# One ACT and one DVE instruction for both masks of a channel tile

## The chip, the cores and the metric

The kernel runs on one core of a Trainium2 chip. The metric is the device time of one execution in microseconds (us); lower is better. The engines have short names: PE is TensorE, DVE is VectorE, ACT is ScalarE, POOL is GpSimd, SP is SyncE.

## The reference

A block of a network with adaptive layer norm: a Mamba-2 layer over 1024 tokens and 512 features, then a small projection with signed weights. Only the part that the change touches matters here. The 1024 tokens are cut into chunks of 128, and the layer has 128 heads of 64 channels in 8 groups.

```python
A_cum = jnp.cumsum(A_dt, axis=-1)
L = jnp.exp(_segsum(A_dt))            # per head and chunk, 128 x 128, lower triangle
Y_diag = jnp.einsum('bzlhn,bzshn,bhzls,bzshp->bzlhp', Cc, Bc, L, xch)
...
Y_off = jnp.einsum('bzlhn,bzhpn,bhzl->bzlhp', Cc, prev, jnp.exp(A_cum))
Y = (Y_diag + Y_off).reshape(b, s, H, P) + hs * D[None, None, :, None]
g = y * jax.nn.silu(gate)
```

For each head the mask exp(A_cum[l] - A_cum[s]) is multiplied by C B^T, which all heads of a group share, and the product multiplies the scaled inputs.

## The kernel before

**Work and stages.** The kernel has 32 units: 8 groups (g), and in each of them four units c = 0 to 3. A unit is a block of 512 channels (8 heads) times half of the tokens (512, which is 4 chunks): c = 0 and 1 are the first block of the group, c = 2 and 3 the second; even c is the first half of the tokens (hf = 0), odd c the second. The first and the last group are written out, and groups 1 to 6 are one loop. Every engine has its own program in which the order of the work is written out by hand, and semaphores tie the programs together.

**The first part of a unit.** TensorE makes the gate projections (gate_proj, L638), transposes the inputs (L717) and makes the chunk states and the output projection of the unit before. A gate projection has to wait for the convolution of the channels before it (v_conv) and, for z = 2, for an earlier SiLU of a gate (a_gate), which frees the PSUM bank.

**The second part, where the change is.** It runs over the four channel tiles j of the unit, two heads each. For tile j:

- PE: exp_a(j) (L692) spreads exp(A_cum) into a bank, diff(2j) and diff(2j+1) (L677) put the differences of A_cum in banks 2 and 3. These run one tile ahead. Then come C times the states (L801, "yo") which waits for v_t1 of tile j-1, and the masked product (L814, "yd") which waits for v_m. For tile 0 it waits also until the part sum of the unit before is read out of its bank (L1340 or L1343). After it come input projections (L488 to L490) for the next unit.
- ACT: ea(j) (L1100), a copy out of PSUM that for j >= 2 waits for POOL's sum of tile j-2 (p_t3). Then decays(j) (L1086): two Relu (L1092) that take the two differences out of PSUM to lm, and two Exp in place (L1095). After it come g_hi and the square of tile j-1, one step of the convolution (L920), a weight part (L890), and at the end of the unit the SiLU of the next inputs (L1037) and gates (L1050).
- DVE: mix (L1430) multiplies lm of a head by cbm, the masked C B^T. Then t2(j) (L1460, `yt`) and t1(j) (L1465, `ea`), g_lo of tile j-1 (L1442) and the convolution (L1241). The mixes of tile j+1 stand ahead of t2 and t1 of tile j.
- POOL: for tile j the sum (L1634, waits for t1(j)), the product with the gate (L1637), the sum of squares (L1629) and the low part of a weight (L1549).

lm has four slots of 512 columns, so the two heads of a tile lie next to each other: slots 0 and 1 for even j, 2 and 3 for odd j.

Of the kernel before, what the change touches and what calls it, by code (L numbers as in the profile page):

```python
# [15 lines left out]
HALF = 512  # L16
# [9 lines left out]
def adaln_mamba_ffn(nc: bass.Bass, x, w_in, w_out, blk_par, bc_par, dt_bias, a_log, c_col, w_mod,  # L26
                    w_ffn, b_ffn, ident_in, keep_in, rows_in, cols_in, sel_in, out):
    F, R, BF = mybir.dt.float32, mybir.dt.float32r, mybir.dt.bfloat16
    ALU, ACT = mybir.AluOpType, mybir.ActivationFunctionType

    ctx = ExitStack()
    with ctx:
        def sb(name, shape, dt=F):
            return ctx.enter_context(nc.sbuf_tensor(name, shape, dt))

        def sem(name):
            return ctx.enter_context(nc.semaphore(name))
# [12 lines left out]
        lm = sb("lm", [128, 4, HALF])  # L50
# [9 lines left out]
        cbm = sb("cbm", [128, TOK])  # L60
# [26 lines left out]
        def scratch(name, shape, dt=F):  # L87
# [24 lines left out]
                   for i in range(2)]  # L112
# [15 lines left out]
        a_silu, a_bcsilu, a_l = sem("a_silu"), sem("a_bcsilu"), sem("a_l")  # L128
        a_fall, a_ea, a_hi, a_sq = sem("a_fall"), sem("a_ea"), sem("a_hi"), sem("a_sq")
# [3 lines left out]
        v_cbm, v_bl, v_m, v_t1, v_t2, v_lo = (sem("v_cbm"), sem("v_bl"), sem("v_m"), sem("v_t1"), sem("v_t2"),  # L133
                                              sem("v_lo"))
# [4 lines left out]
        def ge(eng, s, value):  # L139

            if not (isinstance(value, int) and value <= 0):
                eng.wait_ge(s, value)


        def toks(hf, z=0, n=NZ):
            return slice(hf * HALF + z * CHUNK, hf * HALF + (z + n) * CHUNK)

        def chunk(z):
            return slice(z * CHUNK, (z + 1) * CHUNK)

        def slot(hf, z):

            return (NZ * hf + z) % (NZ + 1)
# [21 lines left out]
        def par(b, j, k):  # L175

            i = j * (TAPS + 3) + k
            return bpar[:, b, i:i + 1]
# [5 lines left out]
        def flat(t, a, b):  # L184

            return t[:, a:b, :].rearrange("p a n -> p (a n)")
# [88 lines left out]
        def late_bank(z):  # L275

            return (7, 0, 1)[z - 1]
# [204 lines left out]
        def _(te):  # L482
# [167 lines left out]
            def unit(g, c, last, first):  # L650
                u, nb, hf = UPG * g + c, 2 * g + c // 2, c % 2
# [28 lines left out]
                def exp_a(j):  # L680

                    if j == 0:
                        te.wait_ge(d_par[par_], 208 * (nb + 1))
                    if j == 0:
                        te.wait_ge(a_gate, 4 * u + 3)
                    elif j == 1:
                        if not first:
                            out_read(g, c, 0 if end else 2)
                    else:
                        te.wait_ge(a_ea, 4 * u + j)  # L690
                    e = 32 * EA_ROWS[j]
                    nc.tensor.matmul(bank[ea_bank(c, j)][:, :], sel[e:e + SROWS, :], rt[par_][e:e + SROWS, :],  # L692
                                     start=True, stop=True).then_inc(t_ea, 1)
# [92 lines left out]
                for j in range(NCT):  # L786
                    if j < NCT - 1:
                        exp_a(j + 1)
                        diff(2 * j + 2)
                        diff(2 * j + 3)  # L790

                    if j == 0:
                        te.wait_ge(v_prev, sb0 + 3)
                        if c in (0, 3):
                            ge(te, v_var, 2 * g + (1 if c else 0))
                        if c == 0:
                            te.wait_ge(v_bl, 2 * g + 1)
                    else:
                        te.wait_ge(v_t1, 4 * u + j)
                    for z in range(1 - hf, NZ):  # L800
                        lst = nc.tensor.matmul(bank[6][:, chunk(z)], prev[:, slot(hf, z), j * 128:(j + 1) * 128],  # L801
                                               ct[:, toks(hf, z, 1)], start=True, stop=True)
                    lst.then_inc(t_yo, 1)

                    te.wait_ge(v_m, 8 * u + 2 * j + 2)
                    if j == 0:
                        if not end and not first:
                            out_read(g, c, 3)
                    else:
                        te.wait_ge(v_t2, 4 * u + j)  # L810
                    for z in range(NZ):
                        for i in range(2):
                            h = 2 * j + i
                            lst = nc.tensor.matmul(bank[5][64 * i:64 * i + 64, chunk(z)],  # L814
                                                   xdt[:, z, h * HDIM:(h + 1) * HDIM], lm[:, h % 4, chunk(z)],
                                                   start=True, stop=True)
                    lst.then_inc(t_yd, 1)
                    if j == 0:
                        n = project_step(0, 0)
                    if j >= 1 and end:  # L820
                        if j >= 2:
                            te.wait_ge(v_row, 2)
                        out_proj(u - 1, j, late_bank(j))
                    if j == 0 and end:

                        te.wait_ge(a_gate, 4 * UNITS)
                        for v in range(2):
                            for k in range(NK):
                                te.wait_ge(v_diag, NK * v + k + 1)
                                lst = nc.tensor.matmul(bank[v][:, k * 128:(k + 1) * 128], ones[:, :],  # L830
                                                       (ga_row, gb_row)[v][:, k * 128:(k + 1) * 128],
                                                       start=True, stop=True)
                            lst.then_inc(t_row, 1)
                    n = project_step(j + 1, n)
                    if j == 2 and c < 3:
                        gate_proj(g, c + 1, 0)
# [13 lines left out]
            u = UNITS - 1  # L850
# [33 lines left out]
        def _(se):  # L884
            act = nc.scalar.activation
# [176 lines left out]
            def unit(g, c, last, first):  # L1062
                u, nb, hf = UPG * g + c, 2 * g + c // 2, c % 2
# [22 lines left out]
                def decays(j):  # L1086


                    for h in (2 * j, 2 * j + 1):
                        se.wait_ge(t_diff, 8 * u + h + 1)  # L1090
                        ge(se, t_yd, 4 * u + h // 2 - 1)
                        act(lm[:, h % 4, :], bank[2 + h % 2][:, :], ACT.Relu, scale=-1.0).then_inc(a_fall, 1)  # L1092
                    for h in (2 * j, 2 * j + 1):
                        se.wait_ge(a_fall, 8 * u + h + 1)
                        act(lm[:, h % 4, :], lm[:, h % 4, :], ACT.Exp, scale=-1.0).then_inc(a_l, 1)  # L1095

                def exp_a(j):
                    se.wait_ge(t_ea, 4 * u + j + 1)
# [83 lines left out]
        def _(ve):  # L1182
            vec = nc.vector
            tt, stt, ts = vec.tensor_tensor, vec.scalar_tensor_tensor, vec.tensor_scalar
# [140 lines left out]
            two = lambda t: t.rearrange("p (v k) -> p v k", v=2)  # L1325
# [39 lines left out]
            def unit(g, c, last, first):  # L1365
                u, nb, hf = UPG * g + c, 2 * g + c // 2, c % 2
# [60 lines left out]
                nv, hv = (nb, 1) if hf == 0 else (nb + 1, 0)  # L1427
                pv = (c // 2) if hf == 0 else (c // 2 + 1) % 2

                def mix(h):  # L1430

                    ve.wait_ge(a_l, 8 * u + h + 1)
                    if h == 0 and c == 0:
                        ve.wait_ge(v_cbm, 2 * g + 2)
                    tt(lm[:, h % 4, :], lm[:, h % 4, :], cbm[:, toks(hf)], ALU.mult).then_inc(v_m, 1)  # L1435

                def lower_g(j):
                    ve.wait_ge(a_hi, 4 * u + j + 1)
# [4 lines left out]
                        ALU.mult, ALU.subtract).then_inc(v_lo, 1)  # L1443

                mix(0)
                mix(1)
                if not first and not end:
                    accumulate(u, g1, b1, h1, 3)
                if hf == 0:
# [1 line left out]
                cols = slice(0 if hf else CHUNK, HALF)  # L1451
                for j in range(NCT):
                    if j < NCT - 1:
                        mix(2 * j + 2)
                        mix(2 * j + 3)

                    ve.wait_ge(t_yd, 4 * u + j + 1)
                    ge(ve, a_sq, 4 * u + j - 1)
                    ge(ve, v_lo, 4 * u + j - 1)
                    stt(yt[:, j % 2, :], xc[:, j, :], par(c // 2, j, SKIP), bank[5][:, :], ALU.mult, ALU.add)\  # L1460
                        .then_inc(v_t2, 1)

                    ve.wait_ge(t_yo, 4 * u + j + 1)
                    ve.wait_ge(a_ea, 4 * u + j + 1)
                    tt(ea[:, j % 2, cols], bank[6][:, cols], ea[:, j % 2, cols], ALU.mult).then_inc(v_t1, 1)  # L1465
                    if j >= 1:
                        lower_g(j - 1)
                    for item in items[j]:
                        conv(item, item_bank(n), nv, hv, g + 1, pv)
                        n += 1  # L1470
                    if end:
                        if j == 0:
                            gate_rows()
                        else:
                            accumulate(u, g1, b1, h1, j, late_bank(j))
                        for t in ((), (), (0,), (1,))[j]:
                            first_residual(t)
# [244 lines left out]
```

## Time and profile before

| what | value |
|---|---|
| median of 3 runs | 1830.39 us (1828.36 to 1834.19) |
| the profiled execution | 1830.74 us |
| its span, first to last instruction | 1828.9 us |
| granted TensorE clock, mean over the span | 0.985 |
| PE busy | 1740.6 us, 95% |
| DVE busy | 1309.0 us, 72% |
| ACT busy | 1014.8 us, 55% |
| POOL busy | 945.9 us, 52% |

Durations and waits come from the profiled execution, which lies 0.35 us above the median; 1.84 us of it lie outside the span. A start time is counted from the first instruction. In the rows, "idle before" or a bracket is the time in which the engine had nothing to run before this instruction, and the arrow names what ended it.

### The profile page before, as it was taken

The page shows a single profiled execution, that of the slowest core. Times are in us where ns is not written, and L with a number is a line of the kernel's source. Part 1 is how long each engine was busy: PE and PEld are TensorE (multiplying, and loading weights), DVE is VectorE, ACT ScalarE, POOL GpSimd, SP SyncE. Part 2 cuts the span into 40 slices and gives each one's busy share as a digit, 9 for nine tenths or more (in the row PEclk, how much of TensorE's full clock was granted, in tenths as well). Part 3 has the DMA queues.
Part 4 walks back from the last instruction along what each step waited for, and adds up shares of the span by engine and source line. Part 5 has one row for each costly group of instructions (what it writes and reads, how often), then busy time and mean ns, then how long its engine had stood idle before and what let it go on. Part 6 is the DMA issues. An engine that isn't in the chain of part 4 may idle for free.

```text
span 1828.9 us, 31129 instructions
## 1 busy us (share of the span) xinstructions
PE 1740.6 (95%) x9656; PEld 1332.9 (73%) x9656; DVE 1309.0 (72%) x2175; ACT 1014.8 (55%) x1709; POOL 945.9 (52%) x723
## 2 busy tenths in 40 slices
PE   6789999999999999999999999999999999999966
PEld 5567777777777777777777777777777777777745
DVE  4766677667866677766777678666777667766788
ACT  6566554565646565565545656465656655565532
POOL 1355464555536465454645555355654546455563
PEclk9899999999999999999999999999999999999988
DMA  6312121121202121121211212121211212111131
GB/s 226 106 39 67 61 67 44 48 63 53 73 28 67 50 71 52 31 68 60 67 45 48 63 53 70 31 73 44 72 52 30 73 56 67 44 50 61 35 98 58
DMA packets 80784, 112.65 MB, mean 62 GB/s; under 512 B 28384, under 2 KB 32480, under 8 KB 79712
## 3 DMA queue, kind: packets, MB, share of 16 engines
q1 hardware_dynamic: 63040, 78.50, 14.1%
q10 hardware_dynamic: 17568, 31.99, 5.2%
q8 instruction: 88, 1.44, 0.3%
q14 instruction: 88, 0.72, 0.1%
HBM read 88.16 MB, written 22.29 MB: 60 GB/s over the span
## 4 chain that ended last, share of the span: by engine, by line
issue 46%; POOL 33%; PE 11%; DVE 4%; ACT 3%; DMA 1%; SPq 1%; POOLq 1%; ACTq 0%; DVEq 0%
POOL yt L1634 9%; POOL ssq L1629 6%; POOL wg_lo L1549 4%; POOL prev L1615 3%; POOL wo_lo L1549 3%; POOL wx_lo L1549 3%; PE bank L488 3%; POOL yt L1637 3%; PE bank L490 2%; PE bank L489 2%; PE bank L663 1%; PE bank L729 1%; DMA raw_w<-w_in_dram 1%; PE bank L862 1%; DMA gate<-w_mod_dram 0%
## 5 line engine op out<-in xcount | busy, mean ns | idle before, releaser
L1634 POOL TENSOR_TENSOR yt<-yt,ea 128x384 f32<-128x384 f32 (+1 forms) x128 | 189.4, 1480 | 392.4 <-DVE ea L1465 392.4
L1435 DVE TENSOR_TENSOR lm<-lm,cbm 128x512 f32<-128x512 f32 x256 | 186.7, 770 | 169.3 <-ACT lm L1095 169.3
L1241 DVE SCALAR_TENSOR_TENSOR xc<-bank,bpar,xc 128x511 f32<-128x511 f32 (+2 forms) x384 | 285.9, 745 | 6.8
L488 PE MATMUL bank<-h_hi,wg_hi 128*128 128x512 f32 x640 | 262.9, 411 | 21.6 <-ACT gate L1050 9.2
L490 PE MATMUL bank<-h_hi,wg_lo 128*128 128x512 f32 x640 | 251.8, 393 | 0.0
L489 PE MATMUL bank<-h_lo,wg_hi 128*128 128x512 f32 x640 | 250.7, 392 | 0.0
L488 PE MATMUL bank<-h_hi,wx_hi 128*128 128x512 f32 x512 | 210.5, 411 | 2.2 <-DVE bt L1241 2.2
L1615 POOL TENSOR_TENSOR prev<-prev,dec 128x512 f32<-128x512 f32 x96 | 102.0, 1062 | 204.6 <-DVE prev L1381 132.0
L488 PE MATMUL bank<-wo_hi,g_hi 128*128 128x512 f32 x496 | 206.6, 417 | 0.0
L490 PE MATMUL bank<-h_hi,wx_lo 128*128 128x512 f32 x512 | 200.5, 392 | 0.0
L489 PE MATMUL bank<-h_lo,wx_hi 128*128 128x512 f32 x512 | 199.8, 390 | 0.0
L490 PE MATMUL bank<-wo_hi,g_lo 128*128 128x512 f32 x496 | 194.7, 393 | 0.0
L489 PE MATMUL bank<-wo_lo,g_hi 128*128 128x512 f32 x496 | 193.5, 390 | 0.0
L1050 ACT ACTIVATE gate<-bank 128x512 f32<-128x512 f32 x128 | 75.2, 588 | 208.4 <-PE bank L490 97.4
L1100 ACT ACTIVATE ea<-bank 128x512 f32<-128x512 f32 x128 | 76.4, 597 | 183.0 <-PE bank L692 132.8
L1637 POOL TENSOR_TENSOR yt<-yt,gate 128x512 f32<-128x512 f32 x128 | 165.9, 1296 | 10.0
L488 PEld LDWEIGHTS bank<-h_hi,wg_hi 128*128 128x128 f32 x640 | 121.0, 189 | 64.2 <-ACT gate L1050 14.3
L920 ACT ACTIVATE xc<-bank,bpar 128x512 f32<-128x512 f32 (+1 forms) x128 | 99.2, 775 | 112.2 <-PE bank L490 64.0
L1095 ACT ACTIVATE lm<-lm 128x512 f32<-128x512 f32 x256 | 149.0, 644 | 0.0
L1629 POOL TENSOR_TENSOR ssq<-ssq,sq 128x512 f32<-128x512 f32 x112 | 145.4, 1298 | 2.6 <-ACT sq L1119 2.6
L814 PE MATMUL bank<-lm,xdt 128*64 128x128 f32 x2048 | 140.6, 280 | 5.4 <-DVE part L1343 4.4
L1549 POOL TENSOR_TENSOR wg_lo<-raw_w,wg_hi 128x512 fp32r<-128x512 f32 x80 | 112.9, 1411 | 56.4 <-ACT wg_hi L890 56.2
(192 smaller groups left out, 3693.6 us busy)
## 6 DMA issues: line engine op xcount, KB each, us to landing
raw_w<-w_in_dram SPq DMA_DIRECT2D x145, 256.0 KB, 2.6
raw_w<-w_out_dram SPq DMA_DIRECT2D x64, 256.0 KB, 2.6
part_d<-part ACTq DMA_DIRECT2D x64, 256.0 KB, 2.0
part<-part_d ACTq DMA_DIRECT2D x58, 256.0 KB, 2.7
rt<-rows_d SPq DMA_DIRECT2D x256, 6.0 KB
acc<-x_dram SPq DMA_DIRECT2D x8, 256.0 KB, 6.9
acc<-w_mod_dram SPq DMA_DIRECT2D x2, 1024.0 KB, 6.7
lh<-neg_d SPq DMA_DIRECT2D x128, 6.0 KB
```

Source lines behind the costliest of these rows:

```text
L488: nc.tensor.matmul(out_ap, whi(k), hhi(k), start=(k == 0), stop=False)
L489: nc.tensor.matmul(out_ap, whi(k), hlo(k), start=False, stop=False)
L490: last = nc.tensor.matmul(out_ap, wlo(k), hhi(k), start=False, stop=(k == n - 1))
L814: lst = nc.tensor.matmul(bank[5][64 * i:64 * i + 64, chunk(z)], xdt[:, z, h * HDIM:(h + 1) * HDIM], lm[:, h % 4, chunk(z)], start=True, st ...
L1095: act(lm[:, h % 4, :], lm[:, h % 4, :], ACT.Exp, scale=-1.0).then_inc(a_l, 1)
L1241: stt(dst[:, at], ps[:, 0:HALF - 3 + k], w(k), dst[:, at], ALU.mult, ALU.add)\
L1435: tt(lm[:, h % 4, :], lm[:, h % 4, :], cbm[:, toks(hf)], ALU.mult).then_inc(v_m, 1)
L1549: tt(lo[:, j, :], raw_w[:, s, :], hi[:, j, :].bitcast(F), ALU.subtract).then_inc(p_w, 1)
L1615: tt(prev[:, slot(hf, z + 1), :].rearrange("p (h c) -> p h c", h=BH), prev[:, slot(hf, z), :].rearrange("p (h c) -> p h c", h=BH), d.unsqu ...
L1629: tt(ssq[:, hf, :], ssq[:, hf, :], sq[:, :], ALU.add).then_inc(p_ss, 1)
L1634: tt(yt[:, j % 2, cols], yt[:, j % 2, cols], ea[:, j % 2, cols], ALU.add).then_inc(p_t3, 1)
L1637: tt(yt[:, j % 2, :], yt[:, j % 2, :], gate[:, j, :], ALU.mult).then_inc(p_g, 1)
```

## The change

The two Exp of a tile become one instruction over 1024 columns (both slots of lm), which waits for both Relu. The two products with cbm become one instruction over 2 x 512 columns, in which cbm is read twice by a stride of zero. The semaphores a_l and v_m count one per tile in place of two. The Relu, the number of slots and the order of all the rest stay.

```diff
-                    te.wait_ge(v_m, 8 * u + 2 * j + 2)
+                    te.wait_ge(v_m, 4 * u + j + 1)
...
-                    for h in (2 * j, 2 * j + 1):
-                        se.wait_ge(a_fall, 8 * u + h + 1)
-                        act(lm[:, h % 4, :], lm[:, h % 4, :], ACT.Exp, scale=-1.0).then_inc(a_l, 1)
+                    at = flat(lm, 2 * j % 4, 2 * j % 4 + 2)
+                    se.wait_ge(a_fall, 8 * u + 2 * j + 2)
+                    act(at, at, ACT.Exp, scale=-1.0).then_inc(a_l, 1)
...
-                def mix(h):
+                def mix(j):
-                    ve.wait_ge(a_l, 8 * u + h + 1)
-                    if h == 0 and c == 0:
+                    ve.wait_ge(a_l, 4 * u + j + 1)
+                    if j == 0 and c == 0:
                         ve.wait_ge(v_cbm, 2 * g + 2)
-                    tt(lm[:, h % 4, :], lm[:, h % 4, :], cbm[:, toks(hf)], ALU.mult).then_inc(v_m, 1)
+                    two = lm[:, 2 * j % 4:2 * j % 4 + 2, :]
+                    tt(two, two, cbm[:, toks(hf)].unsqueeze(1).broadcast_to((128, 2, HALF)), ALU.mult).then_inc(v_m, 1)
...
                 mix(0)
-                mix(1)
...
-                        mix(2 * j + 2)
-                        mix(2 * j + 3)
+                        mix(j + 1)
```

## Rows read from the trace of the kernel before

**Rows 1.** The page, part 1: busy time and share of each engine.
```profile
PE 1740.6 (95%) x9656; PEld 1332.9 (73%) x9656; DVE 1309.0 (72%) x2175; ACT 1014.8 (55%) x1709; POOL 945.9 (52%) x723
```

**Rows 2.** Waits of PE over the span: us in total, times, longest.
```profile
PE bank L488 <- ACT gate L1050: 9.2, 20, 2.3
PE bank L488 <- DVE xc L1241: 7.2, 9, 1.0
...
PE bank L814 <- DVE part L1343: 4.4, 7, 0.8
...
PE bank L801 <- DVE ea L1465: 4.0, 3, 2.0
```

**Rows 3.** ACT's timeline, a unit c = 1: start us, us, instruction, idle before.
```profile
1017.24 0.60 ACT L1100 ACTIVATE ea<-bank 128x512 f32<-128x512 f32 x1 [1.12 <-PE bank L692]
1017.74 1.08 ACT L1092 ACTIVATE lm<-bank 128x512 f32<-128x512 f32 x2
1018.69 1.16 ACT L1095 ACTIVATE lm<-lm 128x512 f32<-128x512 f32 x2
...
1023.80 0.60 ACT L1100 ACTIVATE ea<-bank 128x512 f32<-128x512 f32 x1 [1.15 <-POOL yt L1634]
...
1025.25 1.16 ACT L1095 ACTIVATE lm<-lm 128x512 f32<-128x512 f32 x2
```

**Rows 4.** DVE's timeline, the same unit.
```profile
1009.28 0.68 DVE L1340 COPY part<-bank 128x512 f32<-128x512 f32 x1
...
1019.36 1.29 DVE L1435 TENSOR_TENSOR lm<-lm,cbm 128x512 f32<-128x512 f32 x2 [1.50 <-ACT lm L1095]
1020.57 0.74 DVE L1460 SCALAR_TENSOR_TENSOR yt<-xc,bpar,bank 128x512 f32<-128x512 f32 x1
...
1025.93 1.55 DVE L1435 TENSOR_TENSOR lm<-lm,cbm 128x512 f32<-128x512 f32 x2 [0.94 <-ACT lm L1095]
```

**Rows 5.** Groups of instructions by line: count, busy us and mean ns, idle before.
```profile
L1095 ACT ACTIVATE lm<-lm 128x512 f32<-128x512 f32 x256 | 149.0, 644 | 0.0
...
L1041 ACT ACTIVATE bt<-bt 128x1024 f32<-128x1024 f32 x8 | 8.5, 1064 | 0.1
...
L1435 DVE TENSOR_TENSOR lm<-lm,cbm 128x512 f32<-128x512 f32 x256 | 186.7, 770 | 169.3 <-ACT lm L1095 169.3
...
L1241 DVE SCALAR_TENSOR_TENSOR xc<-bank,bpar,xc 128x511 f32<-128x511 f32 (+2 forms) x384 | 285.9, 745 | 6.8
...
L1227 DVE SCALAR_TENSOR_TENSOR xc<-bank,bpar,tail 128x3 f32<-128x3 f32 x64 | 13.7, 214 | 15.8 <-ACT xc L920 15.8
```

**Rows 6.** ACT's timeline at the start: an instruction that waits for the one before it.
```profile
19.14 0.78 ACT L929 ACTIVATE yt<-bank,modc 128x512 f32<-128x512 f32 x1 [0.91 <-PE bank L507]
19.95 0.63 ACT L932 ACTIVATE h_hi<-yt 128x512 fp32r<-128x512 f32 x1
```

**Rows 7.** POOL's timeline, the unit of rows 3.
```profile
1022.00 1.71 POOL L1634 TENSOR_TENSOR yt<-yt,ea 128x512 f32<-128x512 f32 x1 [2.93 <-DVE ea L1465]
```

**Rows 8.** PE's timeline, the unit of rows 3.
```profile
1010.12 1.09 PE L814 MATMUL bank<-lm,xdt 128*64 128x128 f32 x16
...
1035.55 0.50 PE L488 MATMUL bank<-h_hi,wg_hi 128*128 128x512 f32 x1 [0.30 <-ACT gate L1050]
```

**Rows 9.** Timeline of all engines at the end of a unit c = 0.
```profile
986.08 0.58 ACT L1050 ACTIVATE gate<-bank 128x512 f32<-128x512 f32 x1
...
986.72 0.50 PE L488 MATMUL bank<-h_hi,wg_hi 128*128 128x512 f32 x1
```

**Rows 10.** Timeline of all engines, tile 3 of a unit c = 2.
```profile
1075.20 2.66 DVE L1435 TENSOR_TENSOR lm<-lm,cbm 128x512 f32<-128x512 f32 x2 [0.59 <-ACT lm L1095]
...
1075.56 1.75 POOL L1549 TENSOR_TENSOR wo_lo<-raw_w,wo_hi 128x512 fp32r<-128x512 f32 x1
...
1082.19 0.50 PE L488 MATMUL bank<-h_hi,wg_hi 128*128 128x512 f32 x1 [0.86 <-DVE xc L1241]
```

**Rows 11.** PE's timeline, tile 0 of a unit c = 3.
```profile
1110.42 1.09 PE L814 MATMUL bank<-lm,xdt 128*64 128x128 f32 x16 [0.61 <-DVE part L1343]
```

## The prediction

> **What bounds the kernel now.** I read the page's busy shares first: PE is busy 95% of the span, no other engine over 72% [rows 1]. ACT and DVE time saved is thus worth nothing by itself; what counts is when PE is made to wait. The list of PE's waits shows few, and they repeat group by group [rows 2]: for a gate's SiLU (20 times), for a convolution (9 times), for the read-out of the part sum ahead of the masked product (7 times), and in the last unit for t1. Then the timelines of one group, engine by engine, to see what each wait hangs on. In a unit c = 1 [rows 3, 4, 7, 8] the chain is:
>
> PE's diff(2) -> ACT's ea(2), Relu pair, Exp pair -> mixes of tile 2 -> t2(1), t1(1) -> POOL's sum (it had waited 2.93 us for t1) -> ea(3) (it had waited 1.15 us for POOL) -> Relu, Exp -> mixes of tile 3 (0.94 us of waiting for Exp) -> t2(2), t1(2) -> POOL's next sum, product and squares -> ACT's g_hi, square, gate -> PE's gate projection, which waits 0.30 us [rows 8].
>
> The end of a unit is therefore bound by a chain of latencies that passes two Exp and mix pairs, and PE has no slack there. The other units end alike: c = 0 has gate ready at 986.66 and PE starts at 986.72 [rows 9]; c = 2 waits 0.86 us for the convolution behind the same t1(2) [rows 10].
>
> **The change, step by step.** All from an Exp pair's present start, X.
>
> *Now.* The Relu pair starts 0.95 before X (1017.74 and 1018.69) and ends 0.13 after it. The first Exp doesn't need the second Relu, so it starts before that has ended. The first mix starts at X + 0.67 (1019.36), while the second Exp runs; the next DVE instruction starts 1.21 later (1020.57), at X + 1.88 [rows 3, 4].
>
> *After.* The Exp must wait for the second Relu: X + 0.13, plus 0.03 for a wait on the engine's own result (19.14 + 0.78 to 19.95 [rows 6]). It has 1024 columns; the trace has no such Exp, only a SiLU of that size at 1064 ns [rows 5], and I take 1.07. The pair now takes 1.16 [rows 3], an upper bound; 1.05 is my lower one. The mix starts 0.03 later, at X + 1.26. No DVE product of 1024 columns is there either: 745 ns for 511 columns and 214 for 3 make 1.045 ns a column [rows 5]. A pair takes 1.29 and holds the engine 1.21, each mix thus 0.69 and holds it 0.605 [rows 4]; with 0.535 more for 512 columns the merged mix holds it 1.14 (bounds 1.10, and 1.21 if nothing is saved). So the next DVE instruction starts at X + 2.40.
>
> The saving in occupancy is 0.07 on DVE and about 0.09 on ACT, which there goes into the 0.16 for the second Relu. The price is that nothing overlaps: each pair that DVE waits for hands on **0.52 us later** (bounds 0.43 and 0.68). Most pairs are such: DVE waits 169.3 us for this Exp, 1.3 us for each of 128 pairs [rows 5]. Behind the waiting mix stand, in DVE's queue, the part sum's read-out (tile 0), t2 and t1 (the others), so it is they that come late.
>
> What passes to PE, at each place:
>
> 1. End of unit, c = 0 and c = 1: t1(1), POOL's sum and ea(3) come 0.52 later, then Exp at 1025.25 + 0.52, and t2(2) at 2.40 behind it, 1028.17. Now it is 1025.93 + 1.55 - 0.08 = 1027.40 (this pair was held up 0.26 by POOL) [rows 3, 4]. That is 0.77, and PE already waits, or is within 0.06 of it: 16 x 0.77 = 12.3 us.
> 2. c = 2: the pair takes 2.66, for POOL works at the same time [rows 10]. With everything 0.52 later POOL's wo_lo starts at 1076.08, ahead of the merged mix (ready at 1075.20 - 0.67 + 0.52 + 1.26 = 1076.31), which I let wait for POOL's end, 1.29 later: free for t2 at 1077.40 + 1.14 = 1078.54 against 1075.20 + 2.66 - 0.08 = 1077.78. That is 0.76, 8 x = 6.1. Were it not held up, t2 would start at 1077.45, 0.33 earlier than now. Both ends count below.
> 3. Masked product of tile 0, c = 3: PE waits for the part sum, which stands behind the mix [rows 2, 11]: 7 x 0.52 = 3.6. For c = 1 the same read-out ends at 1009.96, 0.16 before PE's product at 1010.12 [rows 4, 8]; at 1009.96 + 0.52 + 0.04 it makes PE wait 0.40: 8 x 0.40 = 3.2.
> 4. End of c = 3: DVE is full of convolutions from tile 2 on, so one pair costs 0.52 and the next gives 0.06 back: 0.46, seven times 3.2. Whether PE feels all of it at the turn of the loop is open (bound 0).
> 5. Once in the first unit, where the masked product waits for the mix, 0.5; the last unit, without projections to hide anything, waits for t1 at tiles 2 and 3 [rows 2]: two passed pairs, 1.1.
>
> Places 1 and 3 add up, since the later chain starts from a later PE. Where PE waits at none of these places, the delay is hidden by the input projections between two masked products (over 4 us each). The DMAs, counts of semaphores and PE's own work stay. Sum: 12.3 + 6.1 + 3.6 + 3.2 + 3.2 + 1.6 = **30.0 us**. On the profiled 1830.74 us that is 1860.7, and on the median, 0.35 lower, 1860.4; I say 1860.
>
> **What the Trainium skill says to this.** A DVE product of two SBUF operands and a POOL instruction hold each other up [rows 10]: the pair takes 2.66 us in place of 1.29. The Trainium skill ("SBUF — State Buffer", section "SBUF: two separate sides") has this as an exclusive lock: who starts first keeps the port pair for its whole instruction. By it place 2 costs 6.1 us; without such a lock it would be 8 x -0.33, and the sum 21. The Trainium skill also says in "Perfetto Trace Analysis", section "Optimizing Scalar/DVE Operations", that larger instructions help a saturated engine, and that where these engines aren't saturated but make others wait, breaking instructions up may let work be done sooner; here neither is saturated and PE waits for them, so it speaks against the change. The sum stands without it.
>
> **Rivals.**
>
> *POOL doesn't hold up the mix of c = 2 (chance 0.20).* Place 2 turns to 8 x -0.33 = -2.6 in place of 6.1, and place 4 is not felt: 30.0 - 8.7 - 3.2 = 18.1, 1848.5. For it: POOL's wo_lo and the mix are only 0.23 us apart there. Against: the same chain delays both, so their order should be the same each time.
>
> *The long mix collides more (0.08).* A mix takes 770 ns on the mean against 690 unhindered [rows 4, 5], so 20 us are lost to POOL now. If a merged mix that holds on twice as long meets a POOL instruction of 1.29 us in each of the 16 ends of place 1, 21 us more come on top: 1881. Against: by my times POOL is free when those mixes are ready.
>
> *Occupancy decides (0.04, faster).* PE's waits are set by how full DVE is. Then the 24 unit ends and 7 read-outs of places 1 to 3 get back two pairs at 0.07 each: 4.3 us, 1826. It decides where DVE has no idle time ahead of a mix; yet it is idle there for 169.3 us in sum [rows 5]. The Trainium skill ("Perfetto Trace Analysis", "Optimizing Scalar/DVE Operations") has such a gain from grouping for a saturated engine only, which by the trace DVE is at tile 3 of c = 3 alone.
>
> *Hidden delay (0.08, on the other side: no change).* If PE's short waits are an artefact of modelled matmul ends, and it has 1 us of slack at the ends of units, 0.77 is swallowed: 1830 to 1832. It decides from a slack of 0.8 on. Against: the same wait of about 0.3 recurs in each group [rows 2], what a real bound looks like.
>
> **How the numbers follow.** The forecast has 0.60, with a range of its own from 1853 to 1868: 0.43 and 0.68 for 0.52 scale the sum to 25 and 39, and I cut the upper end, since both upper bounds assume that merging saves nothing. With the first rival the range that holds 8 in 10 goes from 1845 to 1868. A measurement here tells 0.3% (5.5 us) from no change. Slower: 0.60 + 0.20 + 0.08 = 0.88, and 0.01 of the hidden case that leaks through, 0.89; same 0.07; faster 0.04.
>
> **What would show it.** The Exp at about 1.07 us, starting 0.03 after the second Relu's end; the mix at about 1.22 us (unhindered), starting 1.1 after the Exp; DVE's wait for Exp up from 169 us towards 235 (0.59 more for most of the pairs); PE's busy time unchanged and its waits up by about 30 us, under the same names as in [rows 2], with gate waits of about 1.1 us at c = 1, and a new wait for L1340 at c = 1. The prediction is wrong if the merged Exp or mix takes much less than two halves less one overlap, if t1(1) late doesn't make ea(3) late, if the first rival holds, or if PE's longer waits lower its granted clock, for which I have put nothing.

## The result, and the profile after

The changed kernel takes 1863.02 us (median of 4 runs, 1861.19 to 1864.33), the kernel before 1829.4 us beside it. The ratio is 1.0178, with a 95% interval from 1.0164 to 1.0191: slower by 33.6 us. Forecast were 1860 us, with 1845 to 1868 as the range. The profiled execution took 1864.25 us, its span is 1862.4 us.

The page's part 1 of the changed kernel, beside [rows 1]:

```profile
PE 1749.5 (94%) x9656; PEld 1333.3 (72%) x9656; DVE 1288.7 (69%) x2047; ACT 1016.3 (55%) x1581; POOL 948.6 (51%) x723
```

DVE has 128 instructions less and 20.3 us less work, yet the kernel is slower. PE's busy time grew by 8.9 us and its idle time (span less busy) by 24.6, from 88.3 to 112.9. The group of the merged product (count, busy us and mean ns, idle before):

```profile
L1436 DVE TENSOR_TENSOR lm<-lm,cbm 128x1024 f32<-128x1024 f32 x128 | 167.5, 1308 | 219.4 <-ACT lm L1095 219.4
```

The 186.7 us of products have become 167.5, and the 169.3 us that DVE waited for the Exp have become 219.4 [rows 5]. What DVE saved it waits, and more. All instructions of these two lines, by tile (min, median and max ns, us of the first and the last):

```profile
L1095 ACT ACTIVATE lm<-lm x128: 1056/1060/1064, 109.9 to 1787.3; 128x1024 f32<-128x1024 f32 x128
L1436 DVE TENSOR_TENSOR lm<-lm,cbm x128: 1215/1224/2199, 111.0 to 1788.4; 128x1024 f32<-128x1024 f32 x128
```

PE's waits over the span (us in total, times, longest):

```profile
PE bank L488 <- ACT gate L1050: 16.3, 30, 3.0
PE bank L488 <- DVE xc L1241: 16.0, 24, 1.2
...
PE bank L814 <- DVE part L1343: 8.1, 7, 1.5
...
PE bank L814 <- DVE part L1340: 3.2, 8, 0.4
...
PE bank L801 <- DVE ea L1464: 2.1, 2, 1.8
```

The names are those of [rows 2]. The waits for gates, convolutions and the read-out at L1343 are about twice as large, the last unit's wait for t1 has fallen from 4.0 to 2.1 us, and one is new: the read-out at L1340, 8 times 0.4 us. The chain behind them, in the same unit c = 1 (starts are 17.23 us later than before at its first masked product). ACT:

```profile
1034.97 1.08 ACT L1092 ACTIVATE lm<-bank 128x512 f32<-128x512 f32 x2
1036.09 1.06 ACT L1095 ACTIVATE lm<-lm 128x1024 f32<-128x1024 f32 x1
1041.55 0.60 ACT L1100 ACTIVATE ea<-bank 128x512 f32<-128x512 f32 x1 [1.16 <-POOL yt L1633]
...
1043.16 1.06 ACT L1095 ACTIVATE lm<-lm 128x1024 f32<-128x1024 f32 x1
```

DVE:

```profile
1026.52 0.68 DVE L1340 COPY part<-bank 128x512 f32<-128x512 f32 x1
...
1037.18 1.22 DVE L1436 TENSOR_TENSOR lm<-lm,cbm 128x1024 f32<-128x1024 f32 x1 [1.57 <-ACT lm L1095]
1038.32 0.74 DVE L1459 SCALAR_TENSOR_TENSOR yt<-xc,bpar,bank 128x512 f32<-128x512 f32 x1
...
1044.25 1.23 DVE L1436 TENSOR_TENSOR lm<-lm,cbm 128x1024 f32<-128x1024 f32 x1 [1.51 <-ACT lm L1095]
1045.39 0.74 DVE L1459 SCALAR_TENSOR_TENSOR yt<-xc,bpar,bank 128x512 f32<-128x512 f32 x1
```

PE:

```profile
1027.35 1.09 PE L814 MATMUL bank<-lm,xdt 128*64 128x128 f32 x16 [0.43 <-DVE part L1340]
```

To be read here: the Exp starts 1.12 after the first Relu, where it started 0.95 after it; the product starts 1.09 behind the Exp's start, and the next DVE instruction 1.14 behind that. From the first Relu to DVE's next instruction it is 3.35 us (1034.97 to 1038.32), and was 2.83 (17.74 to 20.57 [rows 3, 4]): 0.52 later. Two such pairs one behind the other, with POOL's sum and ea(3) between them, put t2(2) at 18.04 us after the unit's first masked product (1045.39 - 1027.35); it was 17.28 (1025.93 + 1.55 - 0.08 - 1010.12 [rows 4, 8]). That is 0.76.

**Where the 33.6 us arise.** The distance from the masked product of tile 0 of one unit to that of the next (starts of L814 on PE) is steady from group to group, and sorts the loss by place. Groups 1 to 6, us; the last column also holds the turn of the loop:

| kernel | c=0 to 1 | c=1 to 2 | c=2 to 3 | c=3 to next 0 |
|---|---|---|---|---|
| before | 48.0 | 49.7 | 50.7 | 64.5 |
| after | 49.3 | 50.4 | 51.8 | 65.9 |

One distance of 66.56 in before is left out of the table (the last section tells of it). From c = 3 to c = 0 where the code is written out and doesn't turn, it is 62.9 before and 63.1 after. Summed over all of them the growth is 9.7 us in 8 distances, 6.1 in 8, 8.9 in 8 and 4.9 in 7 (6.9 without that one). With 1.9 us more before the first masked product (from 110.31 to 112.24) and 2.0 more behind that of the last unit (from 87.95 to 89.96) it is 33.5, just what the spans differ by. These last two are not the merge's own for the most part (place 5 below).

### The profile page after: what moved, and what is told of

Its sections match the earlier page's. It is cut to its first block, busy times and chain, and to the rows that moved or that the text cites. A ratio compares the mean times of both kernels' runs of the same rounds, so it can differ in the third digit from the quotient of the medians.

```text
span 1862.4 us, 30657 instructions
## 1 busy us (share of the span) xinstructions
PE 1749.5 (94%) x9656; PEld 1333.3 (72%) x9656; DVE 1288.7 (69%) x2047; ACT 1016.3 (55%) x1581; POOL 948.6 (51%) x723
## 4 chain that ended last, share of the span: by engine, by line
issue 48%; POOL 32%; PE 10%; DVE 4%; ACT 3%; DMA 1%; SPq 1%; POOLq 1%; ACTq 0%; DVEq 0%
POOL yt L1633 9%; POOL ssq L1628 6%; POOL wg_lo L1548 4%; POOL prev L1614 3%; POOL wx_lo L1548 3%; POOL wo_lo L1548 3%; POOL yt L1636 3%; PE bank L488 2%; PE bank L490 2%; PE bank L489 2%; PE bank L663 1%; PE bank L729 1%; DMA raw_w<-w_in_dram 1%; PE bank L862 0%; DMA gate<-w_mod_dram 0%
## 5 line engine op out<-in xcount | busy, mean ns | idle before, releaser
L1633 POOL TENSOR_TENSOR yt<-yt,ea 128x384 f32<-128x384 f32 (+1 forms) x128 | 185.5, 1449 | 422.2 <-DVE ea L1464 422.2
L1436 DVE TENSOR_TENSOR lm<-lm,cbm 128x1024 f32<-128x1024 f32 x128 | 167.5, 1308 | 219.4 <-ACT lm L1095 219.4
L814 PE MATMUL bank<-lm,xdt 128*64 128x128 f32 x2048 | 141.8, 281 | 12.8 <-DVE part L1343 8.1
L1548 POOL TENSOR_TENSOR wx_lo<-raw_w,wx_hi 128x512 fp32r<-128x512 f32 x64 | 93.9, 1473 | 104.0 <-ACT wx_hi L890 104.0
L1628 POOL TENSOR_TENSOR ssq<-ssq,sq 128x512 f32<-128x512 f32 x112 | 146.5, 1308 | 0.7 <-ACT sq L1119 0.7
```

The costliest lines, as they stand in the source:

```text
L1436: tt(two, two, cbm[:, toks(hf)].unsqueeze(1).broadcast_to((128, 2, HALF)), ALU.mult).then_inc(v_m, 1)
L1548: tt(lo[:, j, :], raw_w[:, s, :], hi[:, j, :].bitcast(F), ALU.subtract).then_inc(p_w, 1)
L1628: tt(ssq[:, hf, :], ssq[:, hf, :], sq[:, :], ALU.add).then_inc(p_ss, 1)
L1633: tt(yt[:, j % 2, cols], yt[:, j % 2, cols], ea[:, j % 2, cols], ALU.add).then_inc(p_t3, 1)
```

## The experiments

Ratios are to the kernel before, run in the same job (medians 1830.1 to 1830.7).

**One part alone: the products.** The product is merged as in the change, the decays keep their two Exp:

```
+ve.wait_ge(a_l, 8 * u + 2 * j + 2)
+tt(two, two, cbm[...].broadcast_to((128, 2, HALF)), ALU.mult).then_inc(v_m, 1)
```

> Only the product is merged; the two Exp stay. Theory of the handover: it waits for the second Exp, starts at X + 1.19 and holds DVE 1.14, so the next starts at X + 2.33, 0.45 later: about 25 us over before, 1855, with the loop's turn as before. Rival (both cost by their length): about 17 us over before, 1846. Rival (the Exp's wait for the second Relu is what costs): near before, 1832.

Measured: 1852.25 us (1851.39 to 1853.38), ratio 1.0122 [1.0105, 1.0139]. Its unit c = 1, ACT and then DVE:

```profile
1029.83 1.16 ACT L1095 ACTIVATE lm<-lm 128x512 f32<-128x512 f32 x2
```

```profile
1031.02 1.23 DVE L1436 TENSOR_TENSOR lm<-lm,cbm 128x1024 f32<-128x1024 f32 x1 [1.57 <-ACT lm L1095]
```

With the Exp as it was, the product of both heads can only start when the second Exp is done, 1.19 behind the start of the first; the first product used to start 0.67 behind it. This part alone costs 21.6 of the 33 us; the theory of the handover had 25, its rivals 17 and 2.

**The other part alone: the Exp.** One Exp of 1024 columns, two products:

```
-ve.wait_ge(a_l, 8 * u + h + 1)
+if h % 2 == 0: ve.wait_ge(a_l, 4 * u + h // 2 + 1)
```

> Only the Exp is merged; the two products stay. Theory of the handover: the first product starts at X + 1.24, the pair holds DVE 1.21, so the next starts at X + 2.45, 0.57 later than before and more than in the merged kernel (0.50 measured): 32 us of latency, and if the turn of the loop is longer because of ACT's program, 5 us more: 1866, the slowest of the three halves. Rival (both instructions cost by their length, half each): about 17 us over before, 1846.

Measured: 1893.03 us (1892.7 to 1893.19), ratio 1.0344 [1.0326, 1.0361]. A miss of 27 us: it costs more than both parts together.

**The wait alone, nothing merged.** As before, but the first product waits for both Exp:

```
-ve.wait_ge(a_l, 8 * u + h + 1)
+if h % 2 == 0: ve.wait_ge(a_l, 8 * u + h + 2)
```

> Nothing is merged: two Exp and two products as before, but the first product of a tile waits until the second Exp is done. Theory of the handover (what is lost is the overlap of the pair): the product starts at X + 1.19 and the next DVE instruction at X + 2.40, as in the merged kernel, so the unit-to-unit distances are those of the merged kernel, about 28 us over before: 1858. The turn of the loop stays as it was before (64.6 us from the masked product of c = 3 to that of the next c = 0, plus 0.3), since ACT's program is the same. Rival (a long instruction costs by itself, or collides more with POOL): under 10 us over before, below 1840. Rival (occupancy of DVE and ACT decides): no change, 1829 to 1831, since neither does less or more work.

Measured: 1886.91 us (1878.28 to 1890.1), ratio 1.0299 [1.0266, 1.0333]. The sign is right, the size a miss of 29 us, as with the Exp alone; so it lies in what they share, two separate products behind one wait. DVE, and then POOL, at tile 0 of the unit c = 1:

```profile
1039.00 2.37 DVE L1436 TENSOR_TENSOR lm<-lm,cbm 128x512 f32<-128x512 f32 x2 [2.26 <-ACT lm L1095]
1041.29 0.68 DVE L1340 COPY part<-bank 128x512 f32<-128x512 f32 x1
```

```profile
1039.56 1.26 POOL L1550 TENSOR_TENSOR wx_lo<-raw_w,wx_hi 128x512 fp32r<-128x512 f32 x1 [4.50 <-ACT wx_hi L890]
```

The pair takes 2.37 us in place of 1.29: POOL starts 0.56 behind the first product, and the second runs only when POOL is done. In the changed kernel the same neighbours meet and nothing is lost on DVE:

```profile
1025.38 1.22 DVE L1436 TENSOR_TENSOR lm<-lm,cbm 128x1024 f32<-128x1024 f32 x1 [2.32 <-ACT lm L1095]
```

```profile
1025.94 1.79 POOL L1548 TENSOR_TENSOR wx_lo<-raw_w,wx_hi 128x512 fp32r<-128x512 f32 x1 [4.56 <-ACT wx_hi L890]
```

Here it is POOL that takes 1.79 in place of 1.26. PE's waits in the kernel with the wait alone:

```profile
PE bank L814 <- DVE part L1343: 15.0, 7, 2.3
PE bank L814 <- DVE part L1340: 12.0, 8, 1.5
```

They were 4.4 and nothing [rows 2]. A second effect follows from the longest of them, in a unit c = 3. Windows of PE's stretches around its wait (us; PE, PEld, DVE, ACT, POOL busy; granted clock; DMA):

```profile
1140.00:1143.20 3.20, 3.20 (x20) 2.25 (x18) 1.17 (x3) 3.20 (x8) 0.38 (x1) 1.00 0.40 97
1143.20:1145.20 2.00, 0.07 (x1) 0.00 (x0) 2.00 (x2) 2.00 (x6) 2.00 (x2) 1.00 0.04 11
1146.70:1149.90 3.20, 3.20 (x10) 2.44 (x9) 2.08 (x4) 0.00 (x0) 1.04 (x1) 0.52 0.08 21
1150.30:1153.50 3.20, 3.20 (x16) 2.63 (x15) 1.58 (x4) 0.78 (x1) 1.21 (x1) 1.00 0.34 124
```

PE waits 2.02 us for the read-out, and soon after it works again its granted clock stands at 0.52, that is at 1.2 GHz in place of 2.4 for nearly all of this window, with half the matmuls of the first one. Then it is back at 1.00. This recurs: PE waits 2.0 to 2.3 us at each of the seven read-outs of c = 3, and the windows behind them show 0.52 to 0.73.

**The wait with tile 0 merged.** To test the first of these: the same wait for both Exp, but the two products of tile 0, ahead of the read-out, are one instruction; the other tiles keep two.

```
+if h == 0: tt(lm[:, 0:2, :], lm[:, 0:2, :], cbm[...].broadcast_to((128, 2, HALF)), ...)
+elif h > 1: tt(lm[:, h % 4, :], lm[:, h % 4, :], cbm[:, toks(hf)], ...)
```

> The kernel that waits for both Exp, with the product of tile 0 alone made one instruction. In it, tile 0's pair took 2.4 us: POOL's weight part got in between the two products, PE waited 1.5 (c = 1) and 2.0 us (c = 3) for the part sum, and after the 2.0 us its granted clock was 0.5 for some 3 us. Theory (POOL gets in between, and the long wait costs again through the clock): in one piece the product can't be split, the waits fall to 0.4 and 1.1, the slow stretch goes, and 8 x 1.1 + 7 x (0.9 + 1.6) = 26 us come back: 1860, level with the merged kernel. Rival (the excess comes from the other tiles): under 8 us come back, 1880.

Measured: 1856.44 us (1855.45 to 1859.33), ratio 1.0143 [1.0126, 1.016]. The 30 us are gone. In the distances between masked products 9.2 us come back from c = 0 to 1 and 7.7 from c = 2 to 3, which hold the two read-out waits, and 10.6 from c = 3 to 0, 1.5 each in 7, where the slow windows had been. PE's waits for the read-outs:

```profile
PE bank L814 <- DVE part L1343: 7.4, 7, 1.2
...
PE bank L814 <- DVE part L1340: 2.8, 8, 0.4
```

So the waiting for the second Exp, with tile 0's products in one piece, costs 26 us, and the rest of the miss was a POOL instruction between the two products of tile 0, with what followed from it on PE. With the Exp alone the pair takes 2.38 us at the same place; there tile 0 wasn't merged to try it. It follows too that merging a product that waits for both Exp anyway is a gain at this place: it leaves POOL no gap.

**The turn of the loop.** In the trace of the changed kernel ACT's first instruction after a turn comes late. Before, and after (the bracket is idle time that nothing in the profile ends):

```profile
1149.68 0.60 ACT L1050 ACTIVATE gate<-bank 128x512 f32<-128x512 f32 x1 [2.07 <-issue]
```

```profile
1170.62 0.60 ACT L1050 ACTIVATE gate<-bank 128x512 f32<-128x512 f32 x1 [3.25 <-issue]
```

It is 2.8 to 3.3 us at the five turns after, and 2.1 to 2.4 at four turns before (at the other one ACT waits for PE). PE waits for this gate, 0.90 us in this group. A test that changes ACT's program and no work: the changed kernel with one more wait per tile, which is fulfilled already when the next one is.

```
+se.wait_ge(a_fall, 8 * u + 2 * j + 1)
 se.wait_ge(a_fall, 8 * u + 2 * j + 2)
```

> The merged kernel with one more wait per tile in ACT's program, always fulfilled already, so that ACT's loop body has as many instructions as before. In the merged kernel ACT's first instruction after the turn of the loop comes 2.8 to 3.3 us after its last one (2.1 to 2.4 before), and PE waits for it. Theory that this comes from where the turn falls in ACT's program: the gap goes back to about 2.2 and the distance from c = 3 to the next c = 0 falls from 65.9 to about 65.0: some 5 us less, 1858. Rival (the gap is a consequence of the late chain): stays at 1863.

Measured: 1858.5 us (1858.45 to 1860.74), ratio 1.0155 [1.0138, 1.0172]. The same turn:

```profile
1169.11 0.60 ACT L1050 ACTIVATE gate<-bank 128x512 f32<-128x512 f32 x1 [1.73 <-issue]
```

The distance from c = 3 to c = 0 falls from 65.9 to 65.1 us at each of the five turns, 3.6 us in sum. Behind the last unit's masked product 2.4 more come back (87.52 in place of 89.96), but not from ACT's turns (place 5 below), and the distances from c = 0 and c = 1 grow by 0.2 and 0.1 each. The other runs agree: with the Exp merged and no extra wait, as in the kernel with the Exp alone, the gap is 3.0 to 3.3 us; where ACT's program is that of before, as with the products alone and with tile 0 merged, it is 1.7 to 2.5, and the distance from c = 3 to c = 0 is 65.0 and 65.1 us. That the late turn costs 3.6 us is thus shown; why it hangs on the program is not.

**Which tiles carry the loss.** Both instructions are merged for tiles 0 and 1 only, and for tiles 2 and 3 only (with the extra wait of the kernel above):

```
+MERGED = (0, 1)      # or (2, 3)
+if j in MERGED: ... one Exp
+if h // 2 in MERGED: ... one product
```

> Both instructions are merged for tiles 0 and 1 of each unit only; ACT's program keeps its number of instructions by one more, already fulfilled wait per merged tile. Theory of places: only the read-out of the part sum ahead of the masked product of tile 0 passes on: 8 x 0.43 at c = 1, 7 x 0.54 at c = 3, 0.5 in the first unit, some at the end: about 8 us over before, 1838; the ends of units keep their waits of before (0.3 and 0.3 at c = 1). Rival (every merged pair costs the same): half of the 28 us of the padded kernel, 1844.

> The same for tiles 2 and 3 only, padded alike. Theory of places: the two handovers of the chain through t1(1), POOL's sum and ea(3) are both late: 16 x 0.79 at the ends of c = 0 and 1, 8 x 0.33 to 0.55 at c = 2, 7 x 0.3 to 0.46 at the end of c = 3, 2 in the last unit: about 20 us over before, 1850; PE's product of tile 0 waits as before. Rival (every merged pair costs the same): 1844.

Measured: 1839.51 us (1838.31 to 1840.68), ratio 1.0048 [1.003, 1.0067], for tiles 0 and 1; 1850.87 us (1850.08 to 1850.98), ratio 1.0108 [1.0091, 1.0126], for tiles 2 and 3. Over before they are 8.9 and 20.2 us, 29 together; the fully merged kernel with the extra wait has 28. The theory of places had 8 and 20, its rival 14 for each, which is refuted. PE's waits with tiles 0 and 1 merged:

```profile
PE bank L494 <- ACT gate L1056: 11.3, 20, 2.3
...
PE bank L820 <- DVE part L1355: 8.3, 7, 1.5
...
PE bank L494 <- DVE xc L1253: 7.2, 9, 1.0
```

and with tiles 2 and 3:

```profile
PE bank L494 <- DVE xc L1253: 18.0, 25, 1.3
PE bank L494 <- ACT gate L1056: 15.5, 28, 2.7
...
PE bank L820 <- DVE part L1355: 4.8, 7, 0.8
```

(lines are shifted by 6 to 12: L494 is the gate projection, L820 the masked product.) The two halves of the loss come apart: the early tiles lengthen the waits for the read-out and nearly leave the unit's end alone (the gates' 9.2 us became 11.3, the convolutions' 7.2 stayed), the late tiles the other way round.

**The chain made shorter instead.** If what counts is the latency from the differences to t1, then ACT's ea(j), which stands ahead of each Relu pair and which nobody needs before t1, is in the way. The kernel before, with ea(j) moved behind the Exp pair (but for tile 0 of the last unit); nothing is merged:

```
-exp_a(j + 1)
 decays(j + 1)
+exp_a(j + 1)
```

> Nothing is merged; on ACT the copy ea(j) is moved behind the Relu and Exp of its tile (but for tile 0 of the last unit). If the waits of PE come from the chain through POOL's sum, ea(3) and Exp, this takes ea(3)'s wait for POOL out of it: the Relu of tile 3 starts about 1.6 us earlier, its products are then ready when DVE is done with the convolution, and PE's waits at the ends of c = 0 to 2 and for the part sum at c = 3 go: up to 20 us less than before, about 1812. Rival (DVE's or POOL's own occupancy sets the ends of units): no change, 1828 to 1831.

Measured: 1813.28 us (1810.65 to 1815.06), ratio 0.9908 [0.989, 0.9926]: faster than both kernels. PE's waits:

```profile
PE bank L488 <- ACT gate L1050: 5.4, 9, 2.9
...
PE bank L488 <- DVE xc L1244: 3.3, 8, 0.5
...
PE bank L814 <- DVE part L1346: 1.2, 5, 0.4
```

They were 9.2, 7.2 and 4.4 [rows 2]. At tile 3 of the unit c = 1 DVE no longer waits for the Exp:

```profile
1014.21 2.43 DVE L1438 TENSOR_TENSOR lm<-lm,cbm 128x512 f32<-128x512 f32 x2
```

(POOL holds this pair up.) What left the chain is the copy of 0.60 us and with it the 1.15 us that it waited for POOL at this tile [rows 3]. In what order ACT runs is worth more here than what its instructions take.

**The merged version with the shorter chain.** The same move in the changed kernel, without and with the extra wait of the turn test:

> The merged kernel with the same move. The handover is as late as in the merged kernel (about 0.5 us a pair), but there is slack now: if place, not length, decides, it loses far less against its own unmerged twin than the 33 us that the merged kernel loses: about 1816, 4 to 8 over the twin, of which some 5 may be the turn of ACT's loop. Rival (merging costs by itself wherever it stands): 28 to 33 us over the twin, 1840 or more.

> The merged kernel with ea(j) moved behind the Exp, and with one more, already fulfilled wait per tile in ACT's program. If what the merged kernel still loses there against its unmerged twin is mostly the turn of ACT's loop (2.7 to 3.1 us of gap against 2.2, five times), 3 to 4 us of the 6.7 come back: 1816. Rival (the rest is the late part sum at c = 3, up to 0.9 each time): stays at 1820.

Measured: 1819.97 us (1817.1 to 1822.88), ratio 0.9936 [0.9917, 0.9955], and 1816.94 us (1814.45 to 1820.47), ratio 0.9927 [0.9904, 0.995]. With the copy moved, merging costs 7 us without the extra wait and 4 with it, no longer 33 and 28. The 4 are not clear of the noise: the runs of the two kernels overlap. PE's waits in the first:

```profile
PE bank L488 <- ACT gate L1050: 8.0, 5, 5.7
...
PE bank L814 <- DVE part L1346: 4.7, 7, 0.9
```

Once the chain binds the ends of units less, the waits that the later handover lengthens are those for the read-out of c = 3 (4.7 us in 7, from 1.2) and at the turn; of the gates' 8.0 us, 5.7 is one wait in the start stretch, ahead of the first merged instruction. The distance from c = 0 to c = 1 also grew, from 47.6 to 48.1 us, with no wait in the list to show for it, and that stays open. In neither form does the merged kernel win.

## Why the prediction was right

**The handover, 0.52 us: right.** Every link came as worked out: Exp 1.06 us (forecast 1.07) starting 0.04 behind the Relu pair (0.03), product 1.22 (1.22) holding DVE 1.14 (1.14), next instruction 0.52 later. DVE's wait for the Exp grew by 50.1 us to 219.4, not to 235. Pair by pair in the trace, the wait is 0.56 to 0.59 longer at ten of the sixteen pairs of each of the groups 1 to 6. At the others (tiles 1 and 2 of c = 0, tile 2 of c = 1 and of c = 2, tiles 1 and 3 of c = 3) it changed by -0.2 to 0.3.

**Place 1 (forecast 0.77 per end of c = 0 and c = 1): right.** t2(2) is 0.76 later, and the distance from c = 1 to c = 2, which holds this and nothing else, grew by 0.77 (6.1 / 8). PE's waits there are 0.65 us for the gate and 0.35 for a convolution, where 1.1 for the gate was forecast.

**Place 3 (0.52 at c = 3, 0.40 at c = 1): right.** PE's waits rose from 4.4 to 8.1 us in 7 (0.53 each), and the new one is 3.2 us in 8 (0.40 each). The distance from c = 0 to c = 1 grew by 1.21 (9.7 / 8), which is 0.77 + 0.40 and 0.04 over.

**Place 2 (0.76 at the end of c = 2): right in kind, smaller.** POOL's wo_lo started first and the merged product waited for it, as foreseen. POOL, and then DVE, at tile 3 of c = 2:

```profile
1094.05 1.29 POOL L1548 TENSOR_TENSOR wo_lo<-raw_w,wo_hi 128x512 fp32r<-128x512 f32 x1
```

```profile
1094.28 2.14 DVE L1436 TENSOR_TENSOR lm<-lm,cbm 128x1024 f32<-128x1024 f32 x1 [1.18 <-ACT lm L1095]
1096.34 0.73 DVE L1459 SCALAR_TENSOR_TENSOR yt<-xc,bpar,bank 128x512 f32<-128x512 f32 x1
```

```profile
1100.74 0.50 PE L488 MATMUL bank<-h_hi,wg_hi 128*128 128x512 f32 x1 [1.18 <-DVE xc L1241]
```

POOL ends at 1095.34, and t2 starts 1.00 after that, not 1.14. Measured from the unit's masked product of tile 0 (1059.81 before, 1077.79 after) t2 is 0.57 later (18.55 and 17.98) and PE's gate projection too (22.95 and 22.38). So the place costs 8 x 0.57 = 4.6 us, not 6.1; with the 0.53 of place 3 that makes the 1.1 by which the distance from c = 2 to c = 3 grew. The first rival (POOL doesn't hold the product up, 18 us in sum) is refuted: it had this t2 come 0.33 earlier. The Trainium skill ("SBUF — State Buffer", section "SBUF: two separate sides") says that whoever starts first keeps the shared ports for its whole instruction. The traces agree in both directions: here POOL was 0.23 ahead and DVE took 2.14 in place of 1.22; at 1025.38 above DVE was ahead and POOL took 1.79.

**Place 4 (0.46 at the end of c = 3): half right.** Where the code is written out, the distance grew by 0.2. At the turn of the loop it grew by 1.3: of that 0.7 goes with ACT's late start, which the prediction didn't know of and which the extra wait takes away (3.6 us in five turns, its largest missing term), and 0.6 stays, near the 0.46.

**Place 5 (0.5 in the first unit, 1.1 in the last): the first right, the second not there.** The stretch before the first masked product lost 1.9 us, but 1.4 of it (the first Relu starts at 108.76 in place of 107.33) is there before the first merged instruction runs. From that Relu to the masked product it is 3.48 us and was 2.98: the 0.5 of the forecast. PE before, and after, in the start stretch, and the window behind (columns as above):

```profile
94.51 0.47 PE L488 MATMUL bank<-h_hi,wg_hi 128*128 128x512 f32 x1 [2.33 <-ACT gate L1050]
95.00:100.00 5.00, 4.05 (x21) 3.05 (x21) 2.00 (x4) 0.60 (x1) 3.90 (x2) 1.00 0.44 118
```

```profile
94.35 0.47 PE L488 MATMUL bank<-h_hi,wg_hi 128*128 128x512 f32 x1 [3.01 <-ACT gate L1050]
95.00:100.00 5.00, 4.81 (x19) 3.65 (x17) 0.59 (x1) 0.60 (x1) 3.71 (x2) 0.67 0.51 118
```

After the longer wait the granted clock is 0.67 in this window, before it is 1.00. This doesn't go with the merge: the kernel with only ea(j) moved shows 0.66 there, those with one part alone and with tiles 0 and 1 merged 1.00. Behind the last unit's masked product of tile 0 nothing is lost up to PE's last group of transposes (L507, 68.2 us both times), so the forecast 1.1 didn't come. From there to the end it is 21.9 us in place of 19.8, more than 50 us behind the last merged product. That stretch takes 19.2 to 20.1 us in nine of the ten experiments, merged or not, and 21.8 in the one with only tile 0 merged; what sets it was not taken apart.

**The sum.** 30.0 was forecast, and the spans differ by 33.5. Against the forecast the ends of c = 0 and c = 1 with the new read-out wait are 0.3 over, those of c = 2 with the read-out of c = 3 0.8 under (8.9 for 9.7), the ends of c = 3 1.7 over (4.9 for 3.2: the late turns cost 3.6, and the slow stretch of before, 2.0, is not there), and start and end 2.3 over. That 1860 lies so near 1863 is thus in part luck. The sum lacked the late turns (3.6 us) and 3.5 us at start and end that no merged instruction made, and had 1.5 too much at place 2 and 1.1 in the last unit; and the slow stretch of before, 2.0 us that the prediction didn't foresee, worked the other way. Its signs had PE's waits up by about 30 us at the same busy time; they rose by 24.6, and the busy time by 8.9, of which 4.3 lie in the start and end stretches. The rest of that was not taken apart. *Occupancy decides* (1826) fell: DVE did 20.3 us less and PE waited longer. *Hidden delay* fell: the delays of places 1 and 3 reached PE in full. *The long mix collides more* is refuted in its mechanism too: the product's mean is 1308 ns against 1224 unhindered, 11 us lost over 128, where it was 770 against 690, 20 us over 256 [rows 4, 5]. One instruction meets POOL less often than two with a gap between them.

**What the experiments add.** The loss is made of about 22 us for the merged product, 6 for the merged Exp on top of it (1858.5 - 1852.25), and 4.5 for what the extra wait takes away (1863.0 - 1858.5), of which 3.6 are the late turns. The prediction's cause, lost overlap on a chain that PE waits for, is shown from three sides: the wait for both Exp, with nothing merged but tile 0's products, costs 26 us, the loss splits by tile as the two kinds of wait do, and with the chain shortened the same merging costs 4 to 7.

## What to carry to other kernels

Before two instructions are merged, find out who waits for the first half. If a consumer on another engine starts on it, one instruction costs the overlap (here 0.52 us each time, while 0.07 was saved on one engine and 0.09 on the other), and where the slowest engine waits at the end of that chain, it pays it at each pass. Where engines aren't full and still make the slowest one wait, try the order of instructions first: here moving one copy of 0.6 us, with its wait for POOL, off the chain gave 17 us.

## What the runs showed that was not expected

- **A turn of the loop costs ACT 1.6 to 3.3 us** before its first instruction, and how much depends on the program, not on its work: one fulfilled wait more per tile brought it from 3.25 to 1.73 us in the group shown.
- **After a long wait PE's clock can fall.** The case with 2.02 us is above. In the kernel before there is one, after the wait of 1.79 us at a turn:

```profile
502.09 0.49 PE L488 MATMUL bank<-h_hi,wg_hi 128*128 128x512 f32 x1 [1.79 <-issue]
```

and the window of the stretch behind it, with a granted clock of 0.50, the lower of the two levels:

```profile
503.50:506.00 2.50, 2.50 (x7) 1.95 (x6) 1.20 (x3) 0.85 (x1) 2.49 (x3) 0.50 0.01 3
```

That is the distance of 66.56 in place of 64.5. In the changed kernel the longest wait of PE between the first and the last masked product of groups 1 to 6 is 1.75 us, at a turn, and the window behind it shows 1.00; none of its distances has such a step. So between the first and the last unit the clock's part in the result is that before lost 2.0 us to it and after didn't; at the start it is the other way round (place 5). In the kernel with the wait alone it falls behind waits of 2.0 us and more in seven of seven units, in the one with the Exp alone behind four of seven such waits of 2.1 to 2.5 us. The length of the wait alone doesn't decide: at the start, waits of 2.33 and 2.69 us (before, and tiles 2 and 3 merged) left the clock at 1.00.
- **Two short products behind one wait are worse than one long one** if a POOL instruction is ready: 2.37 us in place of 1.22, since POOL slips in between.
